# Attention of a macaron block: row maxima's scores started a quarter step later, value and query/key projections and the maxima's transpose at other positions of the step

## What is computed

```python
Q = x @ wq + bq;  K = x @ wk + bk;  V = x @ wv + bv
Q, K, V = (a.reshape(B * H, S, D) for a in (Q, K, V))        # B 8, H 16, S 512, D 8
scores = jnp.einsum('bqd,bkd->bqk', Q, K) / jnp.sqrt(D)
attn = jax.nn.softmax(scores, axis=-1)
ctx = jnp.einsum('bqk,bkd->bqd', attn, V).reshape(B, S, E)
out = ctx @ wo + bo + x
out = (out - mean(out)) * rsqrt(var(out) + 1e-5) * gamma + beta
```

## Time and profile before

| | us |
|---|---|
| median of 3 executions | 817.22 (816.66 to 818.12) |
| the profiled execution | 816.08 |
| its span, first to last instruction | 813.9 |
| attention's steps 1 to 26, mean | 12.62 each |
| granted TensorE clock, mean | 0.833 of full speed |

### The profile page before, as it was taken

The page is one execution under the profiler, slowest core; times in us unless marked ns, Lnnn a source line. Parts: engine busy times, 40 slices in busy tenths (PEclk is TensorE's granted clock), DMA queues, the critical chain, the costliest instruction groups (busy, mean ns, idle before and its releaser), DMA issues.

```text
span 813.9 us, 16314 instructions
## 1 busy us (share of the span) xinstructions
PE 646.0 (79%) x5121; PEld 283.7 (35%) x5121; DVE 599.6 (74%) x1550; ACT 458.5 (56%) x1057; POOL 408.8 (50%) x559
## 2 busy tenths in 40 slices
PE   4896577632699999999999999999999776667760
PEld 3643455421222222222222232222223533445540
DVE  4788834446878989999899998999983779844430
ACT  5653222210158878888888888888888544222220
POOL 5576778854523234344343443434211448578763
PEclk9997755665579999999999999999999568755665
DMA  7898444325544454454545545455421213443334
GB/s 197 235 252 230 94 75 65 52 24 144 96 87 115 100 116 122 104 128 104 123 113 111 122 102 125 111 112 122 104 58 40 68 29 92 110 88 67 60 42 116
DMA packets 242983, 86.66 MB, mean 106 GB/s; under 512 B 169992, under 2 KB 235688, under 8 KB 242856
## 3 DMA queue, kind: packets, MB, share of 16 engines
q1 hardware_dynamic: 226048, 73.05, 37.8%
q0 software_dynamic: 12288, 10.49, 8.7%
q10 hardware_dynamic: 4584, 2.39, 1.0%
HBM read 56.23 MB, written 31.49 MB: 108 GB/s over the span
## 4 chain that ended last, share of the span: by engine, by line
PE 30%; DVE 26%; POOL 13%; issue 13%; ACT 7%; DMA 7%; SPq 1%; ACTq 0%; POOLq 0%; DVEq 0%
DVE arena L1122 14%; PE psum L1752 8%; PE psum L1743 8%; POOL sums L692 7%; ACT arena L1453 4%; DMA sums<-sums_sb,sidx 4%; POOL arena L667 4%; PE psum L1728 4%; DVE arena L1135 3%; PE psum L1533 2%; DMA arena<-dispatch_rows,arena 1%; DVE arena L1130 1%; PE psum L1692 1%; DVE arena L939 1%; PE psum L1550 1%
## 5 line engine op out<-in xcount | busy, mean ns | idle before, releaser
L1122 DVE TENSOR_REDUCE arena<-psum 128x2 f32<-128x1024 f32 x256 | 306.0, 1212 | 36.3 <-PE psum L1730 36.3
L1453 ACT ACTIVATE arena<-psum 128x512 f32<-128x512 f32 x512 | 278.3, 598 | 72.1 <-PE psum L1743 71.2
L1743 PE MATMUL psum<-arena 122*128 122x512 bf16 x512 | 164.4, 387 | 7.0 <-ACT arena L1453 3.5
L1752 PE MATMUL psum<-arena 128*32 128x512 f32 x1024 | 138.2, 610 | 0.0
L692 POOL DMA_INDIRECT sums<-sums_sb,sidx x64 | 102.0, 1594 | 41.2 <-issue 19.4
L1728 PE MATMUL psum<-arena 48*128 48x512 bf16 x256 | 88.4, 400 | 17.0 <-DMA arena<-qk_parts 7.9
L784 POOL TENSOR_TENSOR arena<-arena 128x128 f32<-128x128 f32 x30 | 14.0, 466 | 149.5 <-DVE arena L1135 149.5
L1730 PE MATMUL psum<-arena 48*128 48x512 bf16 x256 | 88.4, 401 | 0.0
L1743 PEld LDWEIGHTS psum<-arena 122*128 122x128 bf16 x512 | 42.7, 100 | 130.1 <-ACT arena L1453 123.5
L667 POOL DMA_INDIRECT arena<-dispatch_rows,arena x64 | 64.1, 1002 | 27.9 <-issue 17.9
L1610 PE MATMUL psum<-ident,arena 128*128 128x128 f32 x64 | 25.0, 413 | 54.6 <-DMA arena<-dispatch_rows,arena 54.5
(11 more groups left out here) (152 smaller groups left out, 1178.9 us busy)
## 6 DMA issues: line engine op xcount, KB each, us to landing
ctx<-arena SPq DMA_DIRECT2D x32, 256.0 KB, 2.1
arena<-qk_parts SPq DMA_DIRECT2D x127, 64.0 KB
qk_parts<-arena SPq DMA_DIRECT2D x32, 192.0 KB, 3.8
arena<-qk_parts SPq DMA_DIRECT2D x190, 32.0 KB
arena<-qk_parts SPq DMA_DIRECT2D x63, 96.0 KB
arena<-lists SPq DMA_DIRECT2D x16, 256.0 KB, 3.5
sums<-x_sb SPq DMA_DIRECT2D x16, 256.0 KB, 4.6
arena<-ctx SPq DMA_DIRECT2D x64, 64.0 KB, 2.4
```

The lines of the kernel that those rows point to most:

```text
L1122: dve.tensor_reduce(mx_r[r % 2][:, p:p + 9:8], src, X, ALU.max).then_inc(a_mx, 1)
L1453: act.activation(p_r[tau % NPB], bank[4 + tau % 2][:, :], ACT.Exp, scale=SCALE).then_inc(a_P, 1)
L1743: pe.matmul(bank[4 + tau % 2][:, :], keys, heads(q_st[r], rows, g), start=True, stop=True)\
L1752: ins = pe.matmul(bank[6][32 * g:32 * g + 32, :], v_r[r][:, g, kt, :], p_r[(4 * kt + g) % NPB], start=(kt == 0), stop=(kt == 3), tile_posi ...
```

## The change

Scores for the maxima run 1.75 steps ahead of `scores_t` instead of 2 (`HEAD = 6`: six of tile 1's eight before step 0). `v(n+3)` moves from position 10 to behind the last `pv` of tile n-1 at position 3, and `v_copy` from DVE's slot 4 to slot 1. `maxT(n+1)` moves from position 3 to 7, with `max_copy` behind exponential 7. `qk(n+4)` moves from position 6 to 10, and `qk_copy` from behind exponential 7 to behind exponential 11. SP's order becomes loads, `ctx_store`, `max_rows`, `ctx_load`, `stack_store`. The normalising operations of ACT (L1419, L1426) are spread otherwise; the first two turns for the second ffn's router stand later in step 30. POOL's program is the same.

```diff
+    HEAD = 6
-            uses += [u for u in (("x", n + 4), ("m", n + 1), ("q", n + 4), ("v", n + 3), ("o", n - 2))
+            uses += [u for u in (("x", n + 4), ("v", n + 3), ("m", n + 1), ("q", n + 4), ("o", n - 2))
@@ SP, step
                         stack_load(n + 3, (r + 3) % NBUF)
+                    if mid or n >= 1:
+                        ctx_store(n - 1, (r - 1) % NBUF)
                     if mid or n + 1 < end:
                         max_rows(n + 1, (r + 1) % NBUF)
                     if mid or n >= 1:
-                        ctx_store(n - 1, (r - 1) % NBUF)
+                        ctx_load(n - 1, (r - 1) % NBUF)
                     if mid or n + 4 < end:
                         stack_store(n + 4, r)
-                    if mid or n >= 1:
-                        ctx_load(n - 1, (r - 1) % NBUF)
@@ DVE, ahead of the steps and in them
-                for p in range(8):
+                for p in range(HEAD):
                     row_max(1, 1, p)
-                max_high(1, 1)
-                max_low(1, 1)
...
                     for p in range(8):
-                        if n + 2 < NT:
-                            row_max(n + 2, at(2), p)
+                        ahead, part = divmod(HEAD + p, 8)
+                        if n + 1 + ahead < NT:
+                            row_max(n + 1 + ahead, at(1 + ahead), part)
+                            if part == 7:
+                                max_high(n + 1 + ahead, at(1 + ahead))
+                                max_low(n + 1 + ahead, at(1 + ahead))
...
-                        if p == 4 and n + 3 < NT:
+                        if p == 1 and n + 3 < NT:
                             v_copy(n + 3, at(3))
...
-                    if n + 2 < NT:
-                        max_high(n + 2, at(2))
-                        max_low(n + 2, at(2))
@@ ACT, step
-                        if tau == 3 and n + 1 < NT:
+                        if tau == 7 and n + 1 < NT:
                             max_copy(n + 1, (r + 1) % NBUF)
...
-                        if tau == 7 and n + 4 < NT:
+                        if tau == 11 and n + 4 < NT:
                             qk_copy(n + 4, r)
...
@@ PE, step
-                        if tau == 6 and (mid or n + 4 < end):
+                        if tau == 10 and (mid or n + 4 < end):
                             qk(n + 4, r)
-                        if tau == 10 and (mid or n + 3 < end):
-                            v(n + 3, at(3))
...
-                        if tau == 3 and (mid or n + 1 < end):
+                        if tau == 7 and (mid or n + 1 < end):
                             maxT(n + 1, at(1))
                         if tau == 3 and (mid or n >= 1):
                             pv(n - 1, at(-1), 3)
+                        if tau == 3 and (mid or n + 3 < end):
+                            v(n + 3, at(3))
...
-                        if tau % 4 == 1 and (mid or n + 2 < end):
-                            scores(n + 2, at(2), tau // 2)
-                            scores(n + 2, at(2), tau // 2 + 1)
+                        if tau % 4 == 1:
+                            ahead, p = divmod(HEAD + tau // 2, 8)
+                            if mid or n + 1 + ahead < end:
+                                scores(n + 1 + ahead, at(1 + ahead), p)
+                                scores(n + 1 + ahead, at(1 + ahead), p + 1)
...
-                for p in range(8):
+                for p in range(HEAD):
                     scores(1, 1, p)
```

More of the change, by code:

```diff
@@ L1229, in attention @@
                             x_var((n - 7) // GT)
-                        if n == NT - 2 and p == 1:
+                        if n == NT - 2 and p == 2:
                             xT_copy(0)
@@ L1459, in attention @@
                             ctx_copy(n - 1, (r - 1) % NBUF)
-                        if tau == 7 and n + 4 < NT:
+                        if tau == 11 and n + 4 < NT:
                             qk_copy(n + 4, r)
-                        if tau in (11, 15) and n >= 6 and n % GT == 2:
+                        if tau in (11, 13, 14, 15) and n >= 6 and n % GT == 2:
+                            z_norm(n - 6 + (11, 13, 14, 15).index(tau))
+                        if tau in (7, 15) and n >= 8 and n % GT == 0:
                             for t in (0, 1):
[L1464 to L1467, removed]
+                                x_norm(n - 8 + (tau - 7) // 4 + t)
                         if n == NT - 1 and tau in (6, 14):
@@ L1761, in step @@
                             xT(n + 4, r)
-                        if tau == 6 and (mid or n + 4 < end):
+                        if tau == 10 and (mid or n + 4 < end):
                             qk(n + 4, r)
-                        if tau == 10 and (mid or n + 3 < end):
-                            v(n + 3, at(3))
                         if tau == 14 and (mid or n >= 2):
                             proj(n - 2, at(-2))
-                        if not mid and n == NT - 2 and tau == 2:
+                        if not mid and n == NT - 2 and tau == 6:
                             pe.wait_ge(a_mx, 8 * NT)
                             transposes(ffns[1], 0, 0)
-                        if not mid and (n, tau) in ((NT - 2, 10), (NT - 1, 2), (NT - 1, 10)):
+                        if not mid and (n, tau) in ((NT - 2, 12), (NT - 1, 2), (NT - 1, 10)):
                             g = 2 * (n - (NT - 2)) + tau // 8
```

## The result

| | before | changed |
|---|---|---|
| median, same chip | 817.67 us (816.66 to 819.4) | **849.44 us** (848.24 to 850.02) |
| ratio | | 1.0384, 95% interval 1.0363 to 1.0406 |
| profiled execution / span | 816.08 / 813.9 | 850.02 / 848.0 |
| steps 1 to 26, mean | 12.62 us | 13.97 us |

A forecast was written before the change was run, and what follows sets the result against it. The kernel was taken as near PE's and DVE's limits, with the late `qk` making the loop through POOL bind: +34.6 for 26 steps, -1.4 for the prologue, +33.2 on the 817.22 median, 850 us, range 837 to 862.

The forecast's parts named there:

- The loop through POOL: Attention steps: `qk`, `qk_copy`, `split`, `normal`, next `xT`; late `qk` makes each step 13.95 us, +34.6 over 26 steps.
- `qk`'s phase: Start of `qk` counted from the step's start: 7.96 us, 3.83 later than before, against 2.32 of slack.
- the hand-over from POOL to PE: From the end of POOL's `normal` to PE's `xT`: no row of its own, taken as 0.03 us.
- the end of position 9's wait: PE's second pair of scores at position 9 waits for DVE's second row maximum until phase 7.64.
- The prologue: Before step 0: two row maxima fewer, so the first `xT` starts earlier, -1.4 us.
- SP's loop: SP's loads, context store and loads, parts store and landing: 12.9 us a turn, covered by POOL's loop, counted at nothing.
- The rival's range for it: SP's loop binds and POOL's does not: +7 - 1.4 to +20 - 1.4, 823 to 836 us; chance 0.08.
- The estimate of 2.4 for the landing: The 192 KB parts store by the skill's formula, giving an SP loop of 11.5; rows showed 3.8 us.
- The case in which neither loop binds: Rival, kernel faster: 810 us with steps of 12.41, 792 with all PE-DVE waits gone; chance 0.06.
- The 39.6 us of the earlier trace: PE's weight load for the maxima's scores waited behind a row maximum, 39.6 us in all; the change's target.
- The port wait: DVE's `max_low` took 1.26 us instead of 0.2 once in four steps beside a POOL operation; its new place avoids it.
- The clock: Rival: PE's clock falls with the new idle time, costing over 100 us; 0.04 together with a third loop above 862.

The follow-up runs named there:

- 4: Kernel before with only `v` at position 6 and `qk` at 10, their copies moved with them: 849.24 us, ratio 1.0442.
- 5: Changed kernel with SP's parts store ahead of the context loads again, POOL's program untouched: 848.05 us, ratio 1.0391 to the kernel before.
- 1: Changed kernel with POOL's `center(t+1)`, which holds `normal`, ahead of `split`: 838.35 us, ratio 1.0308 to the kernel before.
- 9: Kernel before with `v` at 6, `qk` at 10, and POOL's `center(t+1)` ahead of `split`: 827.24 us, ratio 1.0142.
- 6: Changed kernel with one more 128x128 POOL operation between `split` and `normal`: 865.89 us, ratio 1.0597 to the kernel before.
- experiment 11: Kernel before with only DVE's reciprocal one slot later, in slot 3: 811.2 us, ratio 0.9925.
- 2: Changed kernel with POOL's `center(t+1)` ahead of `split` and SP's parts store ahead of the context loads: 825.29 us, ratio 1.0128 to the kernel before.
- 10: Changed kernel with `qk` at 8, `maxT` at 6, their copies moved, parts store ahead of the context loads: 812.13 us, ratio 0.9959 to the kernel before.
- 12: Scores 1.75 steps ahead, `maxT` at 5, `qk` at 7, `v` at 10, reciprocal in slot 3, parts store ahead of context loads: 831.94 us, ratio 1.0206.
- experiment 3: Changed kernel with `qk` back at 6, its copy behind exponential 7, `maxT` still at 7: 860.88 us, ratio 1.0583 to the kernel before.
- experiment 8: As experiment 7, with DVE's reciprocal one slot later, in slot 3: 871.93 us, ratio 1.0675 to the kernel before.
- experiment 7: Changed kernel with `qk` at 6, `maxT` at 10, their copies moved, parts store ahead of `max_rows`: 837.5 us, ratio 1.026 to the kernel before.

## Why the prediction was right, and where it was off

**The loop through POOL** was the cause. The late `qk` alone brings the loss (4), SP's order alone neither adds nor removes anything (5), POOL's operations in the other order take the wait away, in the changed kernel and in the other (1, 9), and an operation more in the loop lengthens every step by its own length (6). `qk`'s phase was predicted as 7.96 and is 7.89; from there to `xT` it takes 6.09, predicted 5.99. The missing 0.1 is the hand-over from POOL to PE, taken as 0.03: `normal` ends at 420.29, `xT` starts at 420.41. The mean step came out as 13.97 for 13.95, the 26 of them as +34.9 for +34.6. Inside the step the sum holds as well: position 4 was put at phase 3.45 and is at 3.38, the end of position 9's wait at 7.64 and is at 7.57.

**The prologue**, -1.4, was 1.43. Step 0, for which the sum had no term, gave another 2.04. Its matmuls ran at half clock less long: the granted clock in the five microseconds from 229 on was 0.96 in the changed kernel and 0.50 before (busy time by stretch). Attention's start, 1.87 later, took it back. That the total fits to 0.6 us owes something to these two. How much step 0 can vary by itself is seen in experiment 11, whose program up to there is that of the kernel before: 14.95 for 15.88. By the medians of the same chip the difference is 31.8, where +33.2 was forecast.

**SP's loop**, 12.9 and counted at nothing: nothing was right (5). Its length was under-estimated. Measured without POOL's loop an undisturbed turn is 13.23, since the next load goes out 4.07 after the store's issue and not 3.8, and the mean step is 13.67, since landings scatter up to 5.7 (1). The prediction took the median landing and named the slowest only for a single turn; a loop without slack pays for each late one. The rival's range for it was +6 to +19 on the kernel before; measured on its chip it is +23.9, 5 us more. The estimate of 2.4 for the landing, from the Trainium skill, DMA: Bandwidth & Descriptors, section "Anatomy of one DMA", was not for this case: that section gives its sum for transfers that GpSimd issues, and SyncE issues these. The forecast did not use it.

**The case in which neither loop binds** was given 792 to 810. This was the weakest step: it took all of the freed waits as gained. Measured, it is 825 with the changed positions (2) and 812 with the best of mine (10), 10.8 above and 3.6 below the kernel before on the same chips. The reasons are in the rows: with the changed positions the wait of position 9 behind DVE stays, since it comes from the reciprocal that stands ahead of a row maximum and not from how far ahead the scores run (11), and a projection moved away opens a wait for an exponential (2). The 39.6 us of the earlier trace rows, which the prediction read as what the change goes for, are waits of weight loads; PE itself waited 3.2 us there, and of the total hardly anything went when two kinds of step became shorter (11). The port wait did go, as forecast: `max_low` (L1131) over all 32 tiles, min/median/max ns,

```profile
L1131 DVE TENSOR_TENSOR arena<-arena x32: 174/174/176, 219.3 to 643.8; 128x16 bf16<-128x16 f32 x32
```

where before six of the 32 took 1.27 us. This agrees with the Trainium skill, SBUF — State Buffer, section "Who interferes with whom", that a DVE instruction with two SBUF inputs contends with a GpSimd instruction that reads SBUF. In the changed kernel it saved nothing, since POOL's loop sets all kinds of step; in experiment 10 the kind that had it is 12.61 for 12.78.

**The clock** was named as a rival and stayed up with 1.03 us of idle time in front of `xT`. Experiment 6 shows how near it was: with 1.44 it fell in five steps.

What stays open: of experiment 9's last 11.6 us and experiment 2's 10.8 I have the waits in the rows above, but no run that removes them alone; and a version with the gain of 10 and that of 11 was tried only in one form (12).

## What to carry to other kernels

Where each engine runs its own program in order, follow each tile once around through all engines before moving one of its stages: the time from the moved instruction to whatever the next step opens with, by rows, against the step's length. Here the way took 5.96 us and left a slack of 2.32, `qk` moved by 3.83, and one subtraction told the sign and nearly the size. Then do the same for each shared bank and each DMA queue, since the loop that is hidden behind the first one (SP's), and the bank in which two stages stand next to each other, are what the repair runs into. A loop that has no slack also has to be priced with the late landings of its transfers, not with their median. And ask first of a wait which instruction stands ahead of the one that is waited for: moving DVE's reciprocal by one slot brought as much as the moved stages did with both loops out of the way.

## What the hardware showed that I had not expected

- The granted clock fell in five steps of 27 behind gaps of 1.44 us on PE (experiment 6), and in none of the changed kernel, whose gaps are 1.03. One more POOL operation of 0.4 us so cost 1.5 us more in each of those steps. It fell in other runs too: experiment 3 in four steps, behind gaps of 1.48; experiment 8 in seven behind 1.73 to 1.81; experiment 1 behind 2.34 and 2.48. Each of these falls lasted 3.4 us, and 6.8 behind the gaps of over 3 us in experiments 7 and 8. Most gaps of the same length were followed by none.
- The idle time of a whole step told less than its longest gap: PE was idle 1.58 us in most steps of the changed kernel, 1.03 of it in one gap, and 1.57 to 1.67 in those of experiment 3, 1.48 of it in one.
- A small transfer (`max_rows`, 8 KB) landed 3.34 us after its issue behind a 192 KB store on the same queue (experiment 7), with that store, and 1.89 behind the context's store (experiment 1). The 192 KB store itself landed after 4.0 in the median when it followed two loads directly (experiment 1), 3.7 to 3.8 otherwise.
